# Layer-0 routed feed-forward: rows gathered slot by slot from a list sorted on the chip, its weights held over both passes, its biases by products on TensorE

## What is computed

```
xn     = layernorm(x)
e      = argmax(xn @ router_w + router_b)        one of 8 experts per token
h      = xn @ w1[e] + b1[e]                      1024 wide, halves a and g
y      = (a * sigmoid(g)) @ w2[e] + b2[e]        512 -> 128
x      = x + 0.5 * y
```

## Time and profile before

| | us |
|---|---|
| median of 3 runs | 3355.55 |
| lowest, highest run | 3349.03, 3359.73 |
| profiled execution, its own time | 3350.59 |
| span of the profiled execution | 3348.9 |
| TensorE busy | 2403.8 (72%) |
| VectorE busy | 1590.5 (47%) |
| ScalarE busy | 1083.1 (32%) |
| GpSimd busy | 849.2 (25%) |
| mean granted TensorE clock | 0.837 |

### The profile page before, as it was taken

One profiled execution on the slowest core, in us unless ns is written; L12 is line 12 of the kernel. 1 busy time (PEld: TensorE's weight loads), 2 busy tenths in 40 slices (PEclk: granted clock), 3 DMA queues, 4 the chain that ended last, 5 costly groups with the idle time before them and its releaser, 6 DMA issues. The chain is left out here.

```text
span 3348.9 us, 45143 instructions
## 1 busy us (share of the span) xinstructions
PE 2403.8 (72%) x13128; PEld 1597.5 (48%) x13129; DVE 1590.5 (47%) x3638; ACT 1083.1 (32%) x2400; POOL 849.2 (25%) x759
## 2 busy tenths in 40 slices
PE   2696945953647361098799971495999879889998
PEld 2463533633635360087466650494444435544554
DVE  3466943675257527933333349634111267761110
ACT  1342312422223121064344431263222135563222
POOL 4323433223611361077100010384000112200000
PEclk9997957985578555599899985697999878999999
DMA  7101062033522356066200013265000043310000
GB/s 202 54 20 30 1 171 59 19 97 84 113 56 77 81 109 182 1 132 136 58 1 1 1 38 92 52 144 138 0 0 0 19 100 78 83 43 26 0 0 25
DMA packets 316644, 211.22 MB, mean 63 GB/s; under 512 B 64711, under 2 KB 300171, under 8 KB 313963
## 3 DMA queue, kind: packets, MB, share of 16 engines
q1 hardware_dynamic: 282731, 177.16, 19.5%
q0 software_dynamic: 33792, 32.57, 5.9%
HBM read 147.94 MB, written 61.12 MB: 62 GB/s over the span
## 5 line engine op out<-in xcount | busy, mean ns | idle before, releaser
L159 POOL TENSOR_TENSOR rstd<-ln_t,power 128x4 f32<-128x4 f32 (+1 forms) x96 | 96.9, 1021 | 636.3 <-DVE ln_t L152 635.9
L2286 DVE TENSOR_TENSOR x<-x,s_y 128x512 f32 (+1 forms) x16 | 11.0, 688 | 496.8 <-PE s_y L2365 496.8
L2350 PE MATMUL s_z<-s_ha,s_wt_h 128*128 128x512 f32 x512 | 222.4, 592 | 0.0
L2357 PE MATMUL s_z<-s_hb,s_wt_h 128*128 128x512 f32 x512 | 222.3, 592 | 0.0
L1897 PE MATMUL s_hu<-s_xgt,s_w 128*128 128x128 f32 x768 | 195.3, 399 | 1.7 <-ACT s_xgt L1837 0.9
L2576 DVE TENSOR_REDUCE s_mx<-s_sa 128x2 f32<-128x512 f32 x256 | 167.1, 685 | 61.3 <-PE s_sa L2729 59.9
L2657 ACT ACTIVATE s_e<-s_sc 128x512 f32<-128x512 f32 x256 | 149.6, 599 | 123.9 <-PE s_sc L2745 122.4
L1897 PEld LDWEIGHTS s_hu<-s_xgt,s_w 128*128 128x128 f32 x768 | 186.7, 327 | 3.0 <-issue 3.0
L188 PE MATMUL s_tp<-ident,xn 128*128 128x128 f32 x352 | 71.5, 339 | 152.1 <-DVE xn L178 148.1
L1883 PE MATMUL s_lp<-ident,s_posf 48*128 48x48 f32 x2 | 0.6, 312 | 233.6 <-DVE s_prob L1765 233.6
L1706 POOL DMA_INDIRECT s_xg<-rows_dram,s_from_i x96 | 95.8, 998 | 269.2 <-DVE s_to_i L1769 240.5
(11 more groups left out here) (406 smaller groups left out, 5687.6 us busy)
## 6 DMA issues: line engine op xcount, KB each, us to landing
s_w<-in_L_ffn_W_dram SPq DMA_DIRECT2D x96, 256.0 KB
s_kx<-k_dram SPq DMA_DIRECT2D x16, 576.0 KB
s_qx<-q_dram SPq DMA_DIRECT2D x48, 192.0 KB
s_w<-in_L_ffn_w_dram SPq DMA_DIRECT2D x2, 4096.0 KB, 14.4
s_b<-in_L_ffn_b_dram SPq DMA_DIRECT2D x16, 512.0 KB, 7.1
acc_dram<-s_zero SPq DMA_DIRECT2D x16, 512.0 KB, 6.2
acc_dram<-x SPq DMA_DIRECT2D x4, 2048.0 KB, 9.7
x<-acc_dram SPq DMA_DIRECT2D x16, 512.0 KB, 7.0
```

What stands on the lines that cost most here:

```text
L159: pool.tensor_tensor(core.rstd[:, tiles], core.ln_t[:, 2, tiles], core.power[:, 0:CT], ALU.pow).then_inc(s.scale_ready.sem, 1)
L2350: last = pe.matmul(z[:, o, :], wt["h1"][:, f, o * P:(o + 1) * P], ha[:, f, :], start=f == 0, stop=f == HB - 1)
L2357: last = pe.matmul(z[:, o, :], wt["h2"][:, f, o * P:(o + 1) * P], hb[:, f, :], start=f == 0, stop=f == HB - 1)
```

## The change

- x, its sums, the reciprocal deviation and the negative of mean times that deviation lie together in `core.fields`, 136 numbers per token.
- The weights and constants are held in a `L0Weights` object over both passes and the attention between; only the first pass loads them (`load`). The biases b1 and b2 (the latter halved) are cut into three bfloat16 parts in three partitions, and are added by products with ones on TensorE. w2 is not halved any more: the copy into `ht` scales by 0.5.
- SP stores `core.fields` to `x_dram` (with a row 0 of zeros). No row is scattered ahead of the slots: from each token's place VectorE makes one-hot matrices, 32 products of TensorE turn them into the list of tokens by place, and GpSimd gathers each slot's 128 rows (544 bytes each) from `x_dram` inside the slot loop.
- `fill_xs` waits for that gather and normalises the rows as it copies them. VectorE adds the down-product to the gathered row itself, takes its sums in place, and GpSimd stores the whole row to `y_dram`, which SP loads back into `core.fields`.
- 39 slots instead of 40. The chunks are written out instead of looped.

The core of the diff (the slot index arithmetic, the list and the programs around it):

```diff
         @block.sync
+            if load:
+                sp.dma_start(b_rows[:, 0:WIDE], w["L0_ffn_b1"]).then_inc(b_loaded.sem, 16)
+                sp.dma_start(b_rows[:, WIDE:WIDE + P], w["L0_ffn_b2"]).then_inc(b_loaded.sem, 16)
+                sp.dma_start(w1[:, :, :], w["L0_ffn_w1"].rearrange("e d f -> d e f")).then_inc(w_loaded.sem, 16)
...
+            sp.wait_ge(nmr_ready.sem, nmr_ready.past(0))
+            sp.dma_start(x_dram[1:TOKENS + 1, :].rearrange("(p t) d -> p t d", p=P), core.fields[:, :, :]).then_inc(x_stored.sem, 16)
+            if load:
+                sp.dma_start(w2[:, :, :, :], w["L0_ffn_w2"].rearrange("e (a p) n -> p e a n", p=P)).then_inc(w_loaded.sem, 16)
+                sp.wait_ge(b_cut_done.sem, 1)
+                for a in range(3):
+                    sp.dma_start(b[a:a + 1, :, :], b_cut[:, a, :]).then_inc(b_placed.sem, 16)
             sp.wait_ge(stored.sem, 16 * SLOTS)
             for q in range(4):
+                sp.dma_start(core.fields[:, q * 8:(q + 1) * 8, :],
+                             y_dram[1:TOKENS + 1, :].rearrange("(p t) d -> p t d", p=P)[:, q * 8:(q + 1) * 8, :]).then_inc(loaded_back.sem, 16)
+            sp.wait_ge(loaded_back.sem, 64)
         @block.gpsimd
-            for t in range(TILES):
-                pool.indirect_dma_start(sorted_dram, bass.IndirectOffsetOnAxis(ap=pos_i[:, t:t + 1], axis=0),
-                                        sent[:, t, :], None).then_inc(scattered.sem, 16)
+            pool.wait_ge(x_stored.sem, 32 if load else 16)
+            pool.wait_ge(ids_ready.sem, 1)
+            def gather(i):
+                if i >= 2:
+                    pool.wait_ge(gathered[i % 2].sem, 16 * (i // 2))
+                pool.indirect_dma_start(xg[:, i, :], None, x_dram,
+                                        bass.IndirectOffsetOnAxis(ap=ids[:, i:i + 1], axis=0)).then_inc(gathered[i % 2].sem, 16)
+            for i in range(4):
+                gather(i)
+            pool.wait_ge(to_ready.sem, 1)
             for i in range(SLOTS):
+                if i + 4 < SLOTS:
+                    gather(i + 4)
                 pool.wait_ge(y_kept.sem, y_kept.past(i))
+                pool.indirect_dma_start(y_dram, bass.IndirectOffsetOnAxis(ap=to_ids[:, i:i + 1], axis=0),
+                                        xg[:, i, :], None).then_inc(stored.sem, 16)
         @block.vector
+            def cut_b():
+                dve.wait_ge(b_loaded.sem, 32)
+                dve.tensor_scalar(b_rows[:, WIDE:WIDE + P], b_rows[:, WIDE:WIDE + P], 0.5, None, ALU.mult)
+                dve.drain()
+                dve.tensor_copy(b_cut[:, 0, :], b_rows[:, :])
+                dve.drain()
+                dve.tensor_tensor(b_rest[:, :], b_rows[:, :], b_cut[:, 0, :], ALU.subtract)
...
+            for c in range(CHUNKS):
+                if c + 2 < CHUNKS:
+                    ln_dve(dve, core, s, c + 2, c % 2)
+                if c == 2:
+                    shift()
+                if load and c == 4:
+                    cut_b()
...
+            dve.tensor_tensor(slot_hot[:, :, :], parts[:, 0, :].unsqueeze(2).to_broadcast([P, TILES, SLOTS]),
+                              held.count[:, 0:SLOTS].unsqueeze(1).to_broadcast([P, TILES, SLOTS]),
+                              ALU.is_equal).then_inc(slots_hot.sem, 1)
+            dve.drain()
+            dve.tensor_tensor(slot_id[:, :, 1, :], slot_hot[:, :, :],
+                              held.after[:, :].unsqueeze(2).to_broadcast([P, TILES, SLOTS]), ALU.mult).then_inc(tile_ids.sem, 1)
+            for t in range(TILES):
+                last = dve.tensor_scalar(lane[:, t, :], held.count[:, :], parts[:, 1, t:t + 1], None, ALU.is_equal)
...
-            def bias(i, u):
-                e = dve.value_load(owner_i[0:1, bass.ds(i, 1)], min_val=0, max_val=EXPERTS - 1)
-                dve.wait_ge(h_done.sem, h_done.past(i))
-                dve.tensor_tensor(gb[:, u, :], hg[:, u, :], b1[:, bass.ds(e, 1), HID:WIDE], ALU.add)
-                dve.tensor_tensor(ab[:, u, :], ha[:, u, :], b1[:, bass.ds(e, 1), 0:HID], ALU.add).then_inc(biased.sem, 1)
+            def gate(i, u):
                 dve.wait_ge(h_done.sem, h_done.past(i))
+                dve.wait_ge(sig_done.sem, sig_done.past(i))
+                dve.tensor_tensor(hs[:, u, :], ha[:, u, :], gb[:, u, :], ALU.mult).then_inc(gated.sem, 1)
+            def add(i):
+                dve.wait_ge(y_done.sem, y_done.past(i))
+                xi = xg[:, bass.ds(i, 1), 0:D]
+                dve.tensor_tensor(xi, yp[:, 0:P].unsqueeze(1), xi, ALU.add).then_inc(y_taken.sem, 1)
+            def sums(i):
+                dve.drain()
+                dve.bn_stats(xg[:, bass.ds(i, 1), D:D + 6], xg[:, bass.ds(i, 1), 0:D]).then_inc(y_kept.sem, 1)
             def body(i, u, before, after):
-                if after:
-                    bias(i + 1, 1 - u)
                 if before:
-                    keep(i - 1)
+                    add(i - 1)
                 if after:
                     gate(i + 1, 1 - u)
+                if before:
+                    sums(i - 1)
         @block.scalar
+            def fill_xs(i, u, half, more):
+                act.wait_ge(gathered[u].sem, half * 16 + 16 * (more + 1))
                 act.wait_ge(xt_done.sem, xt_done.past(i - 2))
+                one = bass.ds(i, 1)
+                act.activation(xs[:, u, :], xg[:, one, 0:D], ACT.Identity,
+                               bias=xg[:, one, D + 7:D + 8], scale=xg[:, one, D + 6:D + 7]).then_inc(xs_ready.sem, 1)
...
+            def body(i, u, before, after, half):
                 if after > 2:
+                    fill_xs(i + 3, 1 - u, half, 1 + u)
                 if after > 1:
                     keep_xst(i + 2, u)
                 if after:
                     gate(i + 1, 1 - u)
         @block.tensor
+            for t in range(TILES):
+                if t % CT == 0:
+                    pe.wait_ge(lane_ready.sem, lane_ready.past(t // CT))
+                last = pe.matmul(ha[:, 1, 0:2 * SLOTS], lane[:, t, :], slot_id[:, t, :, :].rearrange("p a n -> p (a n)"),
+                                 start=t == 0, stop=t == TILES - 1)
...
+                pe.wait_ge(sig_done.sem, sig_done.past(i - 2))
+                pe.matmul(hg[:, u, :], held.ones_b[0:3, :], b[:, bass.ds(e, 1), HID:WIDE], start=True, stop=False)
+                pe.matmul(hg[:, u, :], xst[:, u, :], w1[:, bass.ds(e, 1), HID:WIDE], start=False, stop=True).then_inc(g_done.sem, 1)
+                pe.wait_ge(gated.sem, gated.past(i - 2))
+                pe.matmul(ha[:, u, :], held.ones_b[0:3, :], b[:, bass.ds(e, 1), 0:HID], start=True, stop=False)
+                pe.matmul(ha[:, u, :], xst[:, u, :], w1[:, bass.ds(e, 1), 0:HID], start=False, stop=True).then_inc(h_done.sem, 1)
```

More of the change, by code:

```diff
@@ L375, in _ @@
-            pool.wait_ge(copied.sem, copied.past(CHUNKS - 1))
-            for t in range(TILES):
-                pool.indirect_dma_start(sorted_dram, bass.IndirectOffsetOnAxis(ap=pos_i[:, t:t + 1], axis=0),
-                                        sent[:, t, :], None).then_inc(scattered.sem, 16)
-            for n in range(2):
-                pool.wait_ge(sorted_loaded[n].sem, 16 * (1 + 3 * n))
+            if load:
+                pool.iota(count_i[:, :], pattern=[[1, P]], base=0, channel_multiplier=0).then_inc(counts_filled.sem, 1)
+                pool.iota(part_i[:, :], pattern=[[0, 1]], base=0, channel_multiplier=1).then_inc(counts_filled.sem, 1)
+                pool.memset(none[:, :], 0.0).then_inc(none_clear.sem, 1)
+                pool.memset(held.ones_b[:, :], 1.0).then_inc(cleared.sem, 1)
+                pool.memset(held.ones[:, :], 1.0).then_inc(cleared.sem, 1)
+                pool.memset(held.zero[:, :, :], 0.0).then_inc(cleared.sem, 1)
+                pool.memset(held.earlier[:, :], 1.0).then_inc(cleared.sem, 1)
+                pool.wait_ge(cleared.sem, 4)
+                pool.affine_select(out=held.earlier[:, :], in_=held.earlier[:, :], compare_op=ALU.is_gt, fill=0.0,
+                                   base=0, pattern=[[1, P]], channel_multiplier=-1).then_inc(earlier_filled.sem, 1)
@@ L432, in _ @@
             flat = lambda t: t[:, :, :].rearrange("p a b -> p (a b)")
[L433 removed]
+            dve.tensor_tensor_scan(flat(run), flat(tot), flat(held.zero), 0.0, ALU.add, ALU.add)
             dve.memset(start[:, 0:1], 0.0)
@@ L496, in body @@
                 if after:
                     gate(i + 1, 1 - u)
+                if before:
+                    sums(i - 1)
             run_slots(dve, body)
[L500 to L507 removed]
+            add(SLOTS - 1)
@@ L546, in body, with run_act @@
                 act.wait_ge(ht_done.sem, ht_done.past(i))
-                act.activation(ht[:, u, :, :], htp[:, u, :, :], ACT.Copy).then_inc(ht_kept.sem, 1)
-            run_slots(act, body)
+                act.activation(ht[:, u, :, :], htp[:, u, :, :], ACT.Copy, scale=0.5).then_inc(ht_kept.sem, 1)
+            def run_act():
```

(13 more changed lines are left out.)

322 lines of the change are left out of this document (164 added, 158 removed).

## The result

Four runs of the changed kernel took 3510.0 us in the median (3504.8 to 3518.0), four of the kernel before on the same chip 3356.1. The ratio is 1.0463, with a 95% interval of 1.0437 to 1.0490: 154 us slower, where I had said about 104. The profiled execution took 3518.0 us (span 3516.3) with a mean granted clock of 0.833, against 0.837 before.

A forecast was written before the change was run, and what follows sets the result against it. TensorE was taken to bound the slots before, at 3.62 us each. Forecast: -82.6 ahead, -18.2 behind, +204.6 in the slots = +103.8 us, so 3454.4 profiled, 3459 against the median; range 3430 to 3520.

The forecast's parts named there:

- the ring: Slot loops: store, gather, fill, sigmoid, product, statistics wait in a circle, 6.5 us a slot, 34 turns a pass; chance 0.72.
- the gathers are hidden: Rival, slot loops: the circle of waits does not close, TensorE paces at 3.7 us a slot, 3277 us; chance 0.12.
- The low clock: Rival, slot loops: TensorE falls to 1.2 GHz between gathers, 7.2 us a slot, 48 us more, 3507; chance 0.13.
- Ahead of the slots: Stages before each pass's first slot: that slot starts 37.8 us sooner in the first pass, 44.8 in the second; gain 82.6.
- First slot to first store: Start of the slot loop: 15.3 us instead of 13.9, 0.4 for bias products and 1.0 for gate and statistics.
- the landing with its handoff: Slot loop, from a gather's start until ScalarE can copy it: 2.6 us to land plus 0.1 for handoffs.
- The last four slots: End of the slot loop, after gather 38: slots at TensorE's pace, 3 x 3.63 = 10.9 us.
- Behind the slots: From the last add to the next stage: 10.6 us against 19.7, gain 9.1 a pass, 18.2 in all.
- The rest of the kernel: Stages outside the changed parts: untouched beyond x lying in rows of 136 numbers, costed at nothing.
- the pairs of store and gather 1.27 us apart: Sign, GpSimd in the slot loops: stores and gathers 1.27 us apart, a pair each 6.5 us.
- VectorE's product waiting for the sigmoid: Sign, VectorE in the slot loops: its product waits for ScalarE's sigmoid; no size given.
- TensorE under 65% busy: Sign, slot loops: TensorE busy under 65% there, each loop some 245 us long.

The follow-up runs named there:

- shortening it by one link: Changed kernel with GpSimd issuing the gather of slot i+5 ahead of the store of slot i instead of behind it: 3417.0 us, ratio 1.0193.
- letting it span two slots: Changed kernel, gathers four ahead, with VectorE's statistics moved ahead of the gate product: 3450.1 us, ratio 1.0257.
- a quarter less work for TensorE: Changed kernel, gathers four ahead, with the two 512-column bias products of each slot left out: 3480.5 us, ratio 1.0396.
- the first experiment: Changed kernel with each slot's gather issued five slots ahead instead of four, nothing else changed: 3337.0 us, ratio 0.9956.

## Why the prediction was right, and where its sum was off

The mechanism held: opening the ring took 169 us away, shortening it by one link 89, letting it span two slots 65, and a quarter less work for TensorE 25. Of the two rivals that could have gone another way, *the gathers are hidden* was not the case of this kernel. One gather more ahead made it the case, and there its price was off: 3337 us against my 3277, because I had TensorE's slot at 3.7 us and it is 4.53. *The low clock* forecast 3507, nearer to 3510 than my own 3459, but by a way that did not happen: a slot of 7.2 us at 1.2 GHz in place of the ring. In 20 of the first 34 turns no more than 6.9 us passed, and the low clock cost 9 us over the 68 turns. What I held against it does not hold in general either: with three-row products TensorE was busy in 119.6 of 120 us and was granted 0.80.

That the result lies inside 3430 to 3520 is in part luck. The upper end stood for a landing of 3.5 us in every turn; the landings account for a third of what was missing, and the rest came from terms for which the range had left no room.

The page "TensorE: Matmul & The Clock Gate" of the Trainium skill, section "HAM oscillation — how this bites in real kernels", describes a kernel in which long waits for DMAs send the array back to the low clock each time; here it was granted 0.86 and 0.89 over the slot loops with a wait in every turn, so the trace agrees in part only. The rule of the Trainium skill's page "DMA: Bandwidth & Descriptors", section "Rules for kernel authors", to issue early and wait late stands, with an addition that the first experiment shows: early counts in the order of the queues, not in slots. Four slots ahead was not early, five was.

The sum, against the profiled execution (3518.0 measured, 3454.4 predicted, 63.6 short):

- *Ahead of the slots,* gain 82.6 predicted, 88.6 measured. The logits came at 41.3 instead of 43.8 and the compares took 5.3 us instead of 6.4 (5.29 for 32); the list needed 13.6 us from positions to first copy, predicted 14.4.
- *First slot to first store,* the term most off for its size: 15.3 predicted, 18.0 measured in the first pass and 19.1 in the second. I had given the bias products 0.4 us; three slots' pairs of them stand ahead of the first down-product. The first ones run at half speed: a pair of long products takes 2.08 us instead of 1.12. In the second pass the granted clock is 0.50 there (570 to 580); in the first the window reads 1.00, with the same 2.08 us. +6.5.
- *The ring,* 6.5 us predicted, 6.79 in the turn shown; mean 7.09 in the first pass (241.2 us in 34 turns) and 7.00 in the second (238.2). Together 68 turns cost 37 us more than the 442 predicted. Link by link, as means over the turns: the landing with its handoff took 3.01 us where I had 2.7, 21 us in all. From the product over the statistics and the store to the next gather it is 2.73 us where I had 2.59, 10 us. The copies and the sigmoid came out as summed at full clock, 1.18 for 1.2; TensorE's low clock, which I had in a rival and not in the ring, added 9 us (granted 0.50 from 136 to 140 us, in a turn of 8.17). So the mis-sized term is the landing, priced from gathers of another stage: its median was 2.88, and seven gathers of the first pass took 3.4 to 3.7. Only this kernel's own second and third gather, with no store close by, land as that row says. My own range had 3.5 at its end.
- *The last four slots,* 10.9 predicted, 15.2 measured in both passes: the first of them are still turns of 6.3 and 4.4 us, since the pipe has to be let out of the ring. +8.6.
- *Behind the slots,* 10.6 predicted, 11.8 and 12.6 measured: -3.2 of the gain. The loads landed later than I had put them.
- *The rest of the kernel,* costed at nothing, is 15 us longer in this execution (3516.3 - 852.8 = 2663.5 against 2648.1). In the profiles of the eleven experiments the same stages, with the same rows of 136 numbers, take from 2645 to 2661 us, 2656 in the middle. So about 7 of the 15 us are the scatter of single executions; whether the other 8 belong to the longer rows stays open, since only one execution of the kernel before was profiled.

Differences: -6.0 + 6.5 + 37 + 8.6 + 3.2 + 15.4 = 64.7, for the 63.6 that was missing; the last statistics, 0.4 us a pass, are counted both in the slots and behind them, the rest is rounding.

Of the signs I had named, the pairs of store and gather 1.27 us apart (1.29), the long wait of ScalarE for the gathers and VectorE's product waiting for the sigmoid (1.67 us in the turn shown) are there. TensorE under 65% busy is not: 80% and 78%, since its slot is 4.5 us and some are run at half the clock. The slot loops are 274 us long and not 245.

The seven long landings of the first pass are those of slots 5, 18, 22, 31 and 36 to 38, in all six kernels with four gathers ahead or the gather moved ahead of the store. Routing the reference's own inputs shows what is in them: the last slot of an expert is filled up with places that all name row 0, and these seven have 85 to 128 such places; the other last slots (10, 14, 26, 35) have 21 to 52 and land in 2.79 to 3.07 us. That points to the many reads of one row, but no run tried it.

What stays open: whether the store close by is what makes the landing 2.9 us instead of 2.6. Why a fp32 product behind a 16-bit one takes 0.1 to 0.2 us longer is shown as a price only.

## What to carry to other kernels

When a transfer is moved into a loop, follow the program order of every queue from its landing back to its issue: whatever stands behind the landing on an in-order engine, and ahead of the issue on another, closes a circle, and its length divided by the slots that it spans is the floor of the pace. One more transfer issued ahead opens it, and one independent operation moved ahead of a wait makes it span two slots; more engine time does neither. Price an engine's turn with its waits, not by its busy time: VectorE at 2.6 us busy set a pace of 3.95.

## What the runs showed of the hardware that I had not expected

- Products of three rows by 384 columns, with TensorE busy in 119.6 of 120 us, were granted a clock of 0.80; the same number over 128 rows 1.00, with TensorE busy in 108.1 us; the changed kernel without either 0.87, with TensorE busy in 94.9 us. A busy TensorE is not by itself one at full clock.
- A three-row bias product of 512 columns costs 0.5 us, not 0.31, where a fp32 product follows it, and grouping the two of a slot takes back 0.30 us.
- Ahead of VectorE's first bias sum, whose operand is chosen by a number that the engine reads first, 0.63 and 0.94 us of idle time were ended by no engine. Which part of them that reading takes was not tried.
- A gather of 128 rows of 544 bytes landed 2.54 to 2.61 us after its start with no store near (both passes of the changed kernel, second and third gather), 2.9 in the median with a store of the same size issued 1.29 us ahead, and 3.4 to 3.7 where 85 or more of its 128 places name the same row.
